# Writing out the batch loop of a four-layer convolution kernel and re-ordering the passages between its stages

## The reference

```python
# layer 0, channel attention
att = einsum('bcn,bdn->bcd', q, q);  att_sm = softmax(max(att) - att)
x = gamma * einsum('bcd,bdn->bcn', att_sm, q) + x
# layers 1 and 3, a long convolution per channel, by FFT in the reference
k = outer(hx, hy) per channel        # hx, hy from a small MLP with sines
x = irfft2(rfft2(x) * rfft2(k))[..., :L, :L] + x * bias[:, None, None]
# layer 2, Haar transform, two soft-thresholded channel mixes, inverse transform
f1 = haar2d(x)
acc = sum over i of  sign(f4) * relu(abs(f4) - tau[i]),  f4 = einsum(f1 * v[i], conv_w[i])
x = haar2d(acc, inverse=True) + x
```

## Time and profile before

| what | value |
|---|---|
| median of 3 runs | 6691.49 us (6686.42 to 6696.54) |
| the profiled execution's own time | 6684.96 us |
| its span, first to last instruction | 6683.2 us |
| PE busy | 6293.8 us (94%) |
| DVE / ACT / POOL busy | 4013.7 / 3907.3 / 2554.8 us |
| mean granted TensorE clock | 0.976 |
| chain that ended last | PE 89%, DMA 4%, ACT 2%, DVE 2%, issue 2% |
| HBM traffic | 182 GB/s over the span |

### The profile page before, as it was taken

The page is one execution under the profiler, slowest core; times in us unless marked ns, Lnnn a source line. Parts: engine busy times, 40 slices in busy tenths (PEclk is TensorE's granted clock), DMA queues, the critical chain, the costliest instruction groups (busy, mean ns, idle before and its releaser), DMA issues.

```text
span 6683.2 us, 142217 instructions
## 1 busy us (share of the span) xinstructions
PE 6293.8 (94%) x37984; PEld 5492.5 (82%) x37984; DVE 4013.7 (60%) x7165; ACT 3907.3 (58%) x7001; POOL 2554.8 (38%) x2436
## 2 busy tenths in 40 slices
PE   6798799999999999999999999999999999999689
PEld 4495599788988899888998889978898889989579
DVE  1142377556775577655776467755676558866866
ACT  1233466555665566655665556655566557755865
POOL 0000255224552255423553235522455226632952
PEclk9898899999999999999999999999999999999999
DMA  6776655575656656476655756656565665534224
GB/s 193 227 214 213 201 187 186 181 223 178 186 178 201 206 183 187 156 239 189 186 185 171 238 173 186 186 183 218 178 186 177 202 202 168 168 120 140 80 83 129
DMA packets 770829, 1217.29 MB, mean 182 GB/s; under 512 B 78854, under 2 KB 475047, under 8 KB 770568
## 3 DMA queue, kind: packets, MB, share of 16 engines
q1 hardware_dynamic: 623112, 945.68, 48.1%
q10 hardware_dynamic: 147456, 268.50, 10.6%
HBM read 808.13 MB, written 405.73 MB: 182 GB/s over the span
## 4 chain that ended last, share of the span: by engine, by line
PE 89%; DMA 4%; ACT 2%; DVE 2%; issue 2%; POOL 1%; SPq 1%; ACTq 0%; DVEq 0%; POOLq 0%
PE ps L457 26%; PE ps L459 13%; PE ps L524 12%; PE ps L475 8%; PE ps L483 7%; PE ps L467 7%; PE ps L435 6%; PE ps L601 5%; DMA mixed<-x 3%; PE ps L535 3%; PE ps L649 1%; DMA pix<-in_x_pix 1%; ACT x L762 1%; DVE pix L1011 1%; DVE ps L1026 1%
## 5 line engine op out<-in xcount | busy, mean ns | idle before, releaser
L1045 POOL TENSOR_TENSOR mag<-mag,sgn 128x512 f32<-128x512 f32 x896 | 1041.5, 1162 | 2177.5 <-ACT mag L714 2151.7
L1060 POOL TENSOR_TENSOR split_a<-field,split_a 128x512 fp32r<-128x512 f32 x512 | 652.0, 1274 | 1798.8 <-ACT split_a L774 1798.8
L457 PE MATMUL ps<-tab_a,img 128*128 128x256 f32 x4096 | 1234.0, 383 | 6.9 <-issue 6.2
L457 PE MATMUL ps<-tab_b,mid 128*128 128x256 f32 x4096 | 1223.3, 380 | 0.4 <-DVE x L940 0.4
L905 DVE TENSOR_TENSOR held<-ps,v_t 128x512 f32<-128x512 f32 x896 | 619.7, 692 | 650.8 <-PE ps L524 609.6
L459 PEld LDWEIGHTS ps<-tab_a,img 128*128 128x128 f32 x4096 | 785.4, 192 | 109.6
L459 PEld LDWEIGHTS ps<-tab_b,mid 128*128 128x128 f32 x4096 | 778.2, 190 | 105.1
L459 PE MATMUL ps<-tab_a,img 128*128 128x128 f32 x4096 | 791.9, 275 | 0.0
L459 PE MATMUL ps<-tab_b,mid 128*128 128x128 f32 x4096 | 786.8, 274 | 0.0
L457 PEld LDWEIGHTS ps<-tab_a,img 128*128 128x128 f32 x4096 | 705.6, 193 | 83.0 <-issue 7.4
L475 PE MATMUL ps<-s_inv,split_a 128*128 128x256 f32 x4096 | 710.0, 317 | 66.5 <-POOL split_a L1060 37.7
(11 more groups left out here) (98 smaller groups left out, 11131.1 us busy)
## 6 DMA issues: line engine op xcount, KB each, us to landing
pix<-in_x_pix SPq DMA_DIRECT2D x256, 512.0 KB, 3.9
mixed<-x ACTq DMA_DIRECT2D x512, 256.0 KB, 3.1
img<-mixed SPq DMA_DIRECT2D x512, 256.0 KB, 2.7
tab_a<-filt SPq DMA_DIRECT2D x1024, 128.0 KB, 2.8
tab_b<-filt SPq DMA_DIRECT2D x1024, 128.0 KB, 2.8
coef<-res ACTq DMA_DIRECT2D x512, 256.0 KB, 2.0
out<-res SPq DMA_DIRECT2D x512, 256.0 KB, 3.2
pix<-in_x_rows SPq DMA_DIRECT2D x128, 512.0 KB, 4.8
```

What stands on the lines that cost most here:

```text
L457: nc.tensor.matmul(o_ps, src[:, 0, H * half:H * half + H], tab[:, N - 1::-1], start=True, stop=False)
L1045: nc.gpsimd.tensor_tensor(mag[:, a], mag[:, a], sgn[:, a], ALU.mult).then_inc(c_mult, 1)
L1060: nc.gpsimd.tensor_tensor(split_a[:, 1], src, split_a[:, 0].bitcast(F32), ALU.subtract)\
```

## The change

The batch loop is a Python loop, so each batch has code of its own. In the forward stage's drain, the first channel of the inverse stage is begun: ACT and POOL split channels 0 and 1, PE does L475 of channel 0, DVE treats its row; PE's wait for the whole `field` moves from the head of the inverse stage to step 3, and that for `f_res` to step 2. The closing Gram matmul moves from after the drain to its first step. In the two opening steps of a forward stage the Toeplitz product is issued ahead of `product(0)`, and the wait for `i_res` stands between them. The last two forward result tiles lie in `img[:, 2]` and `img[:, 3]` rather than in `res`, and ACT's stores stand last in the drain's steps. SP loads chunk 0 of `coef` at j = 4 of the last steps (into `rows`, now first in `crows`), chunk 1 at j = 11 behind the last output store, and the first two Gram chunks (512 KB each) at j = 5 and 6 rather than at the head of the forward stage. In `inverse_stage(-1)` the two `coef` chunks are loaded before the images and tables.

```diff
-    with eng.Fori(0, B - 2) as b:
+    for b in range(B - 2):
         forward_stage(b, fwd=True, shrink=True, gram=True)
         inverse_stage(b, inv=True, mix=True)
...
-        crows = [split_a[:].rearrange("p a b n -> p (a b n)").bitcast(F32), rows[:],
+        crows = [rows[:], split_a[:].rearrange("p a b n -> p (a b n)").bitcast(F32),
...
+        last_res = [img[:, 2], img[:, 3]]
...
-                if gram:
+                if gram and b <= 0:
                     for buf in range(2):
                         load_pix(b + 2, buf, buf)
...
+                    if tail and j == 4 and (mix or b == B - 2):
+                        for s in coef_out:
+                            sp.wait_ge(s, 16 * (32 * (b + 2)) + 16)
+                            sp.nop(nofuse=True)
+                        load_coef(b + 1, 0, 0)
+                    if tail and j in (5, 6) and b <= B - 4:
+                        if j == 5:
+                            sp.wait_ge(mix_mm, 64 * (b + 2) + 64 + CR)
+                            sp.nop(nofuse=True)
+                        load_pix(b + 3, j - 5, j - 5)
...
-                        if j == 8 and (mix or b == B - 2):
-                            for s in coef_out:
-                                sp.wait_ge(s, 16 * (32 * (b + 2)) + 16)
-                                sp.nop(nofuse=True)
+                        if j == 11 and (mix or b == B - 2):
                             sp.wait_ge(i_mm5, 64 * b + 64 + CR)
                             sp.nop(nofuse=True)
-                            load_coef(b + 1, 0, 0)
                             load_coef(b + 1, 1, 1)
...
-                    if shrink and on[0]:
-                        if isinstance(q, int) and q == 0 and j == 0:
-                            pe.wait_ge(i_res, 64 * b + CR)
-                            pe.nop(nofuse=True)
+                    opening = isinstance(q, int) and q == 0 and j < 2
+                    if shrink and on[0] and not opening:
                         product(0)
                     if fwd and on[0]:
...
                         toeplitz(0, img[:, j], tab_a[:, j]).then_inc(f_mm1, 1)
+                    if shrink and opening:
+                        if j == 0:
+                            pe.wait_ge(i_res, 64 * b + CR)
+                        product(0)
...
+                    if gram and isinstance(q, int) and q == 16 and j == 0:
+                        gram_edge(False).then_inc(gram_done, 1)
+                    if fwd and shrink and isinstance(q, int) and q == 16 and j == 1:
+                        inverse_width(64 * b, 0)
                 quads(pe, 16, 3 if fwd else 0, step)
-                if gram:
-                    gram_edge(False).then_inc(gram_done, 1)
...
-                else:
-                    pe.wait_ge(c_field, 64 * b + 64 + CR)
-                    pe.wait_ge(f_res, (64 * B if isinstance(b, int) and b >= B - 2 else 64 * (b + 2)) + CR)
-                    pe.nop(nofuse=True)
...
+                    head = isinstance(h, int) and h == 0
+                    if on[0] and not (head and j == 0 and b < B - 1):
+                        inverse_width(n, j % 2)
...
+                        if head and j == 2:
+                            pe.wait_ge(f_res, 64 * min(b + 2, B) + CR)
...
+                        if head and j == 3:
+                            pe.wait_ge(c_field, 64 * b + 64 + CR)
...
+                        if draining and j >= 1:
+                            act.wait_ge(f_x1, f0 + 64 + CR)
+                            nc.scalar.activation(last_res[j - 1], halved(ps[:, 3, :]), ACT.Copy).then_inc(f_copied, 1)
...
+                    if fwd and shrink and draining and j == 0:
+                        act.wait_ge(c_field, 64 * b + 64 + CR)
+                        inverse_hi(64 * b, 0)
+                    if fwd and shrink and draining and j == 2:
+                        inverse_hi(64 * b + 1, 1)
+                    if fwd and draining:
+                        store()
...
+                    if fwd and shrink and isinstance(q, int) and q == 16 and j == 3:
+                        inverse_halves(64 * b, 0)
```

More of the change, by code:

```diff
@@ L401, in inverse_stage @@
                         load_coef(0, 1, 1)
+                    for j in range(4):
+                        load_img(j, j)
+                        fwd_tables(j, j)
             def last_shrink(b):
@@ L498, in _, with inverse_width @@
             pe.wait_ge(act_init, 7)
+            def inverse_width(n, bank):
+                pe.wait_ge(i_hi, n + 1 + CR)
+                pe.wait_ge(i_lo, n + 1 + CR)
+                pe.wait_ge(i_mlo, n - 1 + CR)
+                haar_inv(bank, split_a).then_inc(i_mm5, 1)
             def forward_stage(b, fwd, shrink, gram):
@@ L725, in step, with store @@
                         relu(0)
-                    if fwd and on[4]:
+                    def store():
                         d = j - 4
@@ L730, in step @@
                         dst = coef[bass.ds(b + 1, 1), bass.ds(4 * q + d, 1), :, :].rearrange("b o p n -> p (b o n)")
-                        act.dma_start(dst, res[:, d % 2].rearrange("p a n -> p (a n)"))\
-                            .then_inc(coef_out[d % 2], 16)
+                        tile = last_res[d + 2] if draining and j >= 2 else res[:, d % 2]
+                        act.dma_start(dst, tile.rearrange("p a n -> p (a n)")).then_inc(coef_out[d % 2], 16)
+                    draining = isinstance(q, int) and q == 16
+                    if fwd and on[4] and not draining:
+                        store()
                     if fwd and on[2]:
@@ L769, in mix_store @@
                             .then_inc(mixed_out[m % 2], 16)
-                    if on[0]:
-                        act.wait_ge(i_mm5, n + CR)
-                        act.nop(nofuse=True)
-                        nc.scalar.activation(split_a[:, 0],
-                                             field[:, :, bass.ds(4 * h + j, 1), :].rearrange("p a o n -> p (a o) n"),
-                                             ACT.Copy).then_inc(i_hi, 1)
+                    if on[0] and not (isinstance(h, int) and h == 0 and j < 2 and b < B - 1):
+                        inverse_hi(n, 4 * h + j)
                     if on[1]:
@@ L785, in step @@
                         act.wait_ge(i_res, n - 5 + CR)
+                        if isinstance(h, int) and h == 0 and j == 4:
+                            for s in coef_out:
+                                act.wait_ge(s, 16 * 32 * min(b + 2, B) + 16)
                         nc.scalar.activation(img[:, d % 4], halved(ps[:, 2, :]), ACT.Copy).then_inc(i_img, 1)
@@ L915, in step @@
                         scale(0)
+                    if fwd and shrink and isinstance(q, int) and q == 16 and j == 3:
+                        inverse_halves(64 * b, 0)
                     if fwd and on[4]:
                         d = j - 4
-                        mean, detail = res[0:1, d % 2, 0, :], res[0:1, d % 2, 1, :]
+                        draining = isinstance(q, int) and q == 16
+                        tile = last_res[d + 2] if draining and j >= 2 else res[:, d % 2]
+                        mean, detail = tile[0:1, 0, :], tile[0:1, 1, :]
                         dve.wait_ge(f_copied, n - 4 + 1 + CR)
@@ L953, in halved, with inverse_halves @@
                 return t.rearrange("p (a n) -> p a n", a=2)
+            def inverse_halves(n, bank):
+                left, right = ps[0:1, bank, 0:N], ps[0:1, bank, N:2 * N]
+                dve.wait_ge(i_mm5, n + 1 + CR)
+                nc.vector.tensor_copy(detail_row, right).then_inc(i_detail, 1)
+                dve.wait_ge(i_detail, n + 1 + CR)
+                nc.vector.tensor_tensor(right, left, detail_row, ALU.subtract)
+                nc.vector.tensor_tensor(left, left, detail_row, ALU.add).then_inc(i_halves, 1)
             def inverse_stage(b, inv, mix):
```

31 lines of the change are left out of this document (13 added, 18 removed).

## The result

The changed kernel takes 6581.43 us (median of 4 runs, 6577.35 to 6583.48), the kernel before on the same chip 6688.95 (4 runs, 6683.74 to 6696.54): ratio 0.9838, 95% interval 0.9821 to 0.9855. That is 107.5 us or 1.6% faster; forecast was 6584.5, so 3 us off. The profiled executions differ by 6683.2 - 6579.6 = 103.6 us of span.

What follows compares the result with a forecast made beforehand. PE's work bounds the stages; the change shortens only passages and start. Gains 50 + 50.5 + 6 + 0.5 = 107 us from 6684.96 give 6578, plus 6.5 for the runs' median: 6584.5 us, range 6563 to 6620.

Steps and rivals of the forecast that it cites:

- The bound: Inside the stages PE's work sets the time and stays as it is; the change works on passages and start alone.
- Forward to inverse: Seven passages, last turn to fifth L475 group: mean 32.0 falls to 24.8 us, 7.2 each, gain 50.
- some 2 us at most: Forward-to-inverse passage: cost of a shorter 1.2 GHz spell, two groups at 2.07 for 1.19, added to 23.5; 24.8 taken.
- the drain hides less: Rival: channel 1's split or the slow clock leaves 4 gained per forward-to-inverse passage, not 7.2; 22 lost, 6607; chance 0.12.
- Inverse to forward: Six passages, last Toeplitz to product(0) of step 2: 121.9 us falls to 71.4, 11.9 each, gain 50.5.
- Either cure alone is worth little, and the change makes both: Inverse-to-forward passages: branch idleness (4.69 us) and late store (DVE waits 4.97) overlap, so curing only one gains little.
- What moves at no cost: Last steps and drain: moved loads, stores, img tiles and PE waits are covered by slack and cost nothing.
- The start: Into batch 0: loading coef ahead of images and tables shortens PE's 13.31 us wait; gain 6 (3 to 8).
- `last_shrink`: It keeps its head; 0 to 1 us gained, 0.5 taken.
- landing stayed late: Rival, inverse to forward: moved loads still precede the last stores, PE waits at i_res; 20 lost, 6604; chance 0.12.
- rival of fetch stalls in straight code: Rival: each written-out piece is fetched at 4.69 us, up to 42 stalls, 90 slower, 6781; chance 0.04.
- The clock never falls: Rival: full clock in both kinds of passage, 8.5 and about 9 gained each, 118 in all, 6573; chance 0.08.

Runs made afterwards that it cites:

- experiment 9: Changed kernel with ACT's split of channel 1 placed ahead of its copy of the last forward tile in drain step 2: 6563.83 us, ratio 0.9812.
- experiment 5: Changed kernel with product(0) ahead of the Toeplitz product again in the two opening steps: 6594.7 us, ratio 0.9852.
- experiment 2: Kernel before, hardware loop kept, with only the two first coef chunks loaded earlier, between the last output stores: 6679.23 us, ratio 0.9988.
- experiment 1: Kernel before with only the batch loop written out: 6668.07 us, ratio 0.9962.
- experiment 3: Changed kernel with batches 1 to 4 in a hardware loop again (three taken branches): 6595.9 us, ratio 0.9853.
- experiment 8: Changed kernel with the last two forward tiles in res and the Gram closed behind the drain: 6575.8 us, ratio 0.9831.

## Why the prediction held, step by step

**The total.** The mechanism of both passages held, but that the sum came so near is in part luck: forward to inverse gained 5.5 less than forecast, inverse to forward 5.3 more, and 3.4 came from a place that was not in the sum.

**The bound.** PE's work inside the stages stayed as it was, and the gain lies in the passages and the start, but for 4 us. Held.

**Forward to inverse**, forecast a gain of 50, measured 44.5. The places of the first two width products were right to a tenth: 7.4 and 12.9 us after the last `turn` by the working, 7.39 and 12.91 in the trace. What was mis-sized is the term after them, "some 2 us at most" for the clock with 1.3 taken. The third product was reckoned at 16.2 and came at 16.76, at 1.2 GHz; the fourth was reckoned one turn of `split_a` (3.3) later and came 4.33 later, since PE's own slower step had become the longer one. That is batch 0; batches 1, 4 and 6 are like it, batches 2, 3 and 5 have only the second product slow. The fifth stands at 25.6 on average, not 24.8. Batch 6, which has an extra idleness of 1.6 already at the first product, took 27.66. That the gaps ahead of channel 1 were the cause, as the rival "the drain hides less" named it, experiment 9 shows: with the first gap cut from 2.66 to 0.55 us, 13.4 more are gained.

**Inverse to forward**, forecast 50.5, measured 55.8. The 11.4 worked out by the order of the engines is 11.06 (the threshold chain, taken at 4.9 from `product(0)` to that of step 1, took 4.51); the 0.5 allowed for late landings wasn't needed, since the store was issued at 1522.08, over 3 us ahead of the tile that waits for it (1525.19), and landed in time in every batch. The granted clock is 1.00, above the 0.9 named.

**"Either cure alone is worth little, and the change makes both."** Shown for IF, and its numbers are the best lesson of the study. IF in us, each by its own experiment:

| | `coef` load late | `coef` load early |
|---|---|---|
| hardware loop | 121.9 | 112.7 |
| written out | 111.7 | 74.6 |

One cure gives 10.2, the other 9.2, both 47.3, and the Toeplitz ahead brings it to 55.8. (The lower right, experiment 5, also has the moved pixel loads and the work in the drain, so the 47.3 are not the two cures' alone.) The statement was too strong only for the whole time: the loop written out also gives some 13 us elsewhere.

**What moves at no cost.** Right for the changed kernel as it is, wrong as an account of its parts. The early closing of the Gram matmul was given no price; its cover is the tiles in `img`, and without them it costs 22.5. The moved pixel loads were costed as work for SP, but they are part of the cure: experiment 2 shows the wait that comes without them in a sooner passage. That they alone would close it wasn't tried.

**The start**, forecast 6, measured 5.3 (8.4 and 7.8 against experiments 1 and 2, which have the old start and took 466.1 and 465.5). **`last_shrink`**, forecast 0.5, measured 0.1 to its last `turn`. **Left out of the sum:** 3.4 us inside the inverse stages that the hardware loop had cost.

**The rivals.** No landing stayed late (1.0 us in all). Written-out code showed no issue idleness at the heads of its stages, so that no rival of fetch stalls in straight code came true. Instruction packets come there too, one from 1525.15 to 1526.56 us, while PE goes on, and the two pages count fewer of them on queue q8 after the change (106) than before (118). So the rule of the Trainium skill named for the branch holds in both directions here. "The clock never falls" is true of one kind of passage and not of the other; experiment 9 comes near to it in both, with four of seven forward-to-inverse passages still slow in part.

## What to carry to other kernels

Where two late things lie on one another, price them together: each alone shows hardly a gain in its passage, and behind both there may be a third (here the pixels). An edit that lets an engine finish sooner also starts the transfers that hang on it sooner: look for what they collide with, and take edits apart in pairs before calling one of them free. In a drain, two gaps of 1 to 2.7 us cost more than their length (13.4 us gained for 8.3 of idle time), because the matmuls behind them run at the lower clock; the order of two instructions on the engine that feeds PE was worth more than the Toeplitz ahead (13.4 against 8.5 us).

## What was not expected of the hardware

- The idleness at a taken branch depends on what is queued: 5.0 us on average with 1 MB of loads just ahead, 2.7 without (24.9 and 13.7 us in 5 waits), in otherwise the same loop. The difference is when a 16 KB instruction packet is carried; PE starts 1.6 to 1.8 us after that packet's end at every branch.
- A hardware loop costs time even away from its branch: 0.57 us in each inverse stage of the kernel before (305.06 against 304.50 in experiment 1), 0.2 to 0.3 in experiment 3. That it is arithmetic on the loop's register was only argued.
- The mixing ahead of batch 0, the same code in all these runs, ended anywhere between 729.8 us (experiment 8) and 745.7 (experiment 1). A comparison of two single profiles of this kernel has to be made from passage to passage, not from span to span.
